# Attention strips: VectorE's instructions in another order, and one quad's values copied by VectorE in place of ScalarE

## The reference

```
xn   = layernorm(x) * g + b                      # over 48 channels, then shifted by 3 and cut into windows
q, k, v = xn @ qkv_w + qkv_b                     # per window: 49 x 16 for each of 3 heads
attn = softmax(q k^T / 4 + rel_bias)             # 49 x 49 per head
out  = (attn v) @ proj_w + proj_b
x    = x + shift_back(out)                       # first residual
h    = gelu(layernorm2(x) @ fc1_w + fc1_b) @ fc2_w + fc2_b
x    = x + h                                     # second residual
```

## Time and profile before

| | |
|---|---|
| median of 3 runs | 1924.59 us (1921.74 to 1933.83) |
| the profiled execution | 1921.47 us, its span 1919.8 us |
| PE, PEld busy | 1733.5 us (90%), 1054.6 us (55%) |
| DVE busy | 1597.7 us (83%) |
| ACT busy | 1535.9 us (80%) |
| POOL busy | 1244.9 us (65%) |
| mean granted TensorE clock | 0.961 |

### The profile page before, as it was taken

How to read it: one execution, slowest core, us unless ns; L and a number is a source line. 1 busy time by engine, 2 the same in 40 slices (tenths; PEclk the granted TensorE clock), 3 DMA queues, 4 the chain that set the end, 5 groups by cost and what they waited for, 6 DMA issues and landing times. The chain is left out here.

```text
span 1919.8 us, 90636 instructions
## 1 busy us (share of the span) xinstructions
PE 1733.5 (90%) x38184; PEld 1054.6 (55%) x38184; DVE 1597.7 (83%) x2140; ACT 1535.9 (80%) x3090; POOL 1244.9 (65%) x1048
## 2 busy tenths in 40 slices
PE   5899999999999999999999999986999958998996
PEld 3566656565666656666665656651697943333332
DVE  6899889998999999999989899854777757888883
ACT  3788888888888888888888888875666639888891
POOL 5788888888888888888888888762355540221222
PEclk9999999999999999999999999995899975999998
DMA  4343554444443444444344444322588849999994
GB/s 116 89 115 97 152 133 115 106 107 115 100 116 99 117 102 113 109 105 113 98 116 102 117 105 106 85 59 67 134 217 215 216 119 170 245 260 253 253 268 142
DMA packets 233230, 262.27 MB, mean 137 GB/s; under 512 B 167078, under 2 KB 179910, under 8 KB 232710
## 3 DMA queue, kind: packets, MB, share of 16 engines
q1 hardware_dynamic: 217478, 217.48, 47.4%
q0 software_dynamic: 15360, 39.08, 6.8%
HBM read 160.81 MB, written 80.88 MB: 126 GB/s over the span
## 5 line engine op out<-in xcount | busy, mean ns | idle before, releaser
L425 POOL TENSOR_TENSOR shift<-const_b,qmax 113x588 bf16<-113x588 bf16 x256 | 414.1, 1618 | 214.7 <-DVE qmax L520 214.7
L512 DVE TENSOR_TENSOR Ul<-Uf 113x784 bf16<-113x784 f32 x192 | 259.8, 1379 | 0.0
L1501 POOL DMA_DIRECT2D out_rolled<-r_OUT x128 | 64.0, 504 | 268.2 <-DVE r_OUT L1601 268.2
L520 DVE TENSOR_REDUCE qmax<-ps_s 113x12 f32<-113x588 f32 x256 | 195.4, 763 | 50.3 <-PE ps_s L917 46.6
L1347 PE MATMUL conv_ps<-xin,band_now 64*64 64x448 bf16 x2688 | 203.4, 365 | 2.2 <-DVE x_low L1242 2.2
L731 ACT ACTIVATE P<-ps_t 113x588 f32<-113x588 f32 x256 | 170.0, 664 | 36.6 <-PE ps_t L969 34.3
L724 ACT COPY Uf<-ps_m 113x392 f32<-113x392 f32 x384 | 172.8, 485 | 28.7 <-PE ps_m L882 20.8
L1347 PE MATMUL conv_ps<-x_low,band_now 64*64 64x448 bf16 x1344 | 178.1, 352 | 0.0
L741 ACT COPY V<-ps_t 49x192 f32<-49x192 f32 x512 | 169.1, 330 | 9.2 <-PE ps_t L969 3.0
L984 PEld LDWEIGHTS ps_o<-P,V 113*32 113x32 f32 x6144 | 107.8, 109 | 102.7 <-ACT P L731 53.0
L762 ACT ACTIVATE G<-ps_m 128x392 f32<-128x392 f32 x256 | 113.9, 502 | 44.5 <-PE ps_m L1023 44.2
(11 more groups left out here) (246 smaller groups left out, 5339.9 us busy)
## 6 DMA issues: line engine op xcount, KB each, us to landing
xin<-rows_scratch SPq DMA_DIRECT2D x96, 236.0 KB, 3.7
XT<-x_tokens SPq DMA_DIRECT2D x64, 294.0 KB, 3.5
X<-x_windows SPq DMA_DIRECT2D x128, 147.0 KB, 3.4
RS<-rs_scratch SPq DMA_DIRECT2D x128, 147.0 KB, 3.2
XR<-x_windows SPq DMA_DIRECT2D x128, 147.0 KB, 3.2
x_scratch<-x SPq DMA_DIRECT2D x128, 147.0 KB, 3.5
y_scratch<-y POOLq DMA_DIRECT2D x96, 196.0 KB, 2.8
r_RS<-rs_scratch SPq DMA_DIRECT2D x128, 147.0 KB, 4.8
```

What stands on the lines that cost most here:

```text
L425: nc.gpsimd.tensor_tensor(shift[:, j % 2], e, m, ALU.mult).then_inc(S["md"], 1)
L512: nc.vector.tensor_tensor(Ul[:, r, h, :], Uf[:, r, h, :], U[0][:, r, h, :], ALU.subtract).then_inc(S["u_lo"], 1)
L520: nc.vector.tensor_reduce(qmax[:, j % 2, :].rearrange("p (b n) -> p b n", b=2), ps_s[0:R, :, 0:2 * HQ].rearrange("p b (n t) -> p b n t", t ...
```

## The change

ScalarE no longer calls `keep_values(s, 2)`, the copies of quad 2 (the third quad). VectorE makes the same two copies in a new `keep_third(s)`, right behind `divide(s, 0)`, counted by a semaphore of their own, `vev_third`; ScalarE's `exp_scores(s, 2)` waits for it, and TensorE's two waits on copied values are split between the two semaphores by `kept`. On VectorE, `u_low(nxt, 1)` moves from ahead of `subtract_mean(prv)` to behind `square(prv)`, and `u_low(nxt, 2)` from ahead of `query_max(nxt, 1)` to behind it. The number of instructions of every kind stays the same over all engines together.

```diff
--- before.py
+++ after.py
@@ -238,11 +238,15 @@
         x2_margin = sem("x2_margin")
         margins_stored = sem("margins_stored")
         names = ("t_sum t_mean t_cen t_sqr t_var t_ln t_rs xh0 lo0 uu u_hi u_lo s_q mx kb md st ex vev pv lnd rdn nrm "
-                 "proj x1_made x1_lo cen xc sq sq_lo var ln rs xh1 lo1 f1 ge f2 x1_biased x2_made").split()
+                 "proj x1_made x1_lo cen xc sq sq_lo var ln rs xh1 lo1 f1 ge f2 vev_third x1_biased x2_made").split()
         S = {nm: sem(f"{nm}_done") for nm in names}
 
         def halves(ap):
             return ap.rearrange("p (b n) -> p b n", b=2)
+
+        def kept(q):
+
+            return (S["vev"], 2 * (q // 4 * 3 + (0, 1, 2, 2)[q % 4])), (S["vev_third"], 2 * (q // 4 + (q % 4 > 2)))
 
         def of_kind(ap, a):
             return ap.rearrange("p (j a t) -> p a j t", a=2, t=2 * TOK)[:, a]
@@ -522,6 +526,15 @@
                         ps_s[0:R, :, 0:2 * HQ].rearrange("p b (n t) -> p b n t", t=TOK),
                         AX_X, ALU.max).then_inc(S["mx"], 1)
 
+            def keep_third(s):
+
+                if s.real:
+                    q = 4 * s.n + 2
+                    wait(dve, S["st"], q + 1)
+                    wait(dve, S["pv"], q - 1)
+                    for p in range(2):
+                        nc.vector.tensor_copy(*kept_values(p, 2)).then_inc(S["vev_third"], 1)
+
             def divide(s, j):
 
                 if s.real:
@@ -602,14 +615,15 @@
                 first_residual(prv)
                 normalise1(old)
                 divide(s, 0)
+                keep_third(s)
                 u_low(nxt, 0)
-                u_low(nxt, 1)
                 subtract_mean(prv)
                 query_max(nxt, 0)
                 divide(s, 1)
                 square(prv)
+                u_low(nxt, 1)
+                query_max(nxt, 1)
                 u_low(nxt, 2)
-                query_max(nxt, 1)
                 add_bias(prv)
 
             def clear_inputs(tiles, r):
@@ -727,6 +741,8 @@
                 if s.real:
                     q = 4 * s.n + j
                     wait(act, S["st"], q + 1)
+                    if j == 2:
+                        wait(act, S["vev_third"], 2 * (s.n + 1))
                     wait(act, S["pv"], q - 1)
                     nc.scalar.activation(P[:, j % 2].rearrange("p (b n) h t -> p b n (h t)", b=2),
                                          ps_t[0:R, :, 0:2 * SV].rearrange("p b (n c) -> p b n c", c=SV)[:, :, :, 0:HQ],
@@ -784,7 +800,6 @@
                 invert_sums_end(s, 0)
                 u_high(nxt, 2, 0)
                 u_high(nxt, 2, 1)
-                keep_values(s, 2)
                 exp_scores(s, 2)
                 token_root(s.at(3))
                 invert_sums(s, 1)
@@ -930,7 +945,8 @@
                     if j == QUADS // 2:
                         wait(pe, swapped[s.slot(2)], 64 * (s.turn(2) + 1))
                     wait(pe, S["ex"], q)
-                    wait(pe, S["vev"], 2 * q)
+                    for copied in kept(q):
+                        wait(pe, *copied)
                     r = s.slot(2)
                     for k in range(2):
                         for n, (ws, ms) in enumerate(((0, 0), (0, 1), (1, 0))):
@@ -975,7 +991,8 @@
                 if s.real:
                     q = 4 * s.n + j
                     wait(pe, S["ex"], q + 1)
-                    wait(pe, S["vev"], 2 * (q + 1))
+                    for copied in kept(q + 1):
+                        wait(pe, *copied)
                     wait(pe, S["nrm"], q)
                     for k in range(QP):
                         at = TOK * (k ^ j // 2 * 2)
```

## The result

The changed kernel takes 1968.93 us (median of 4 runs, 1966.93 to 1970.53) against 1926.94 us before (median of 4, 1921.74 to 1933.83, the runs made beside it included). The ratio is 1.0218 with a 95% interval of 1.0196 to 1.0241: slower, by 42 us; the interval leaves open whether by more than 2%. The forecast was 1957 us.

The account below looks back on a forecast made before the run. No engine has room, so the loop closing a step (19.68 us), with two equally long branches, bounds the kernel. A step of 20.23 us, +0.55 over about 60 steps, adds 33 us: 1957 us, range 1896 to 1975.

Parts of the forecast that it names:

- The two levers: What sets the step: VectorE's mean subtraction (early is good, forecast 0.73 us earlier) and the second residual (late is bad).
- the likeliest case: Main forecast: last low part and add_bias wait for GpSimd, step 20.23 us, 1957 us, range 1940 to 1975; chance 0.56.
- the other branch: Equally long loop branch: second residual, fourth quad's division, projection; residual forecast to start at 621.18 instead of 620.01.
- All three cases: VectorE/GpSimd turns: GpSimd 0.22 us ahead wins; 0.11 ahead, VectorE wins two instructions; 0.3 behind first of two, GpSimd goes between.
- Rival 1: On VectorE, add_bias goes ahead of GpSimd's low0: step 19.27 us, 1900 us in all, faster; chance 0.20.
- Rival 2: VectorE's last low part slips ahead of GpSimd's squares_low: step 19.00 us, 1884 us in all, faster; chance 0.06.
- Rival 3: Issue order alone decides VectorE/GpSimd turns, so make_shift beats the square: +20 us, 1945 us in all; chance 0.04.
- Rival 4: Mixture: L491 is beaten again, step 19.8 us, or strips alternate between both patterns: 1915 to 1940 us; chance 0.14.
- The copies: Third quad's two copies on VectorE behind the division: 0.62 to 0.70 us, hidden under GpSimd's low1.
- the 1.4 of the bound: Upper limit for the two copies on VectorE, in us; would add some 17 us in all through a later exponential.
- What is late next: Chain from second residual to projection: shrinks from 5.06 to 4.38 us, with the projection starting at 625.56.
- my sum: Whole kernel: step 20.23 against 19.68 us, +0.55 us over about 60 steps, +33 us.

Follow-up runs that it names:

- experiment 5: Changed kernel with the two third-quad copies exchanged, partitions 64 to 112 first: 1964.03 us, ratio 1.0204 to the kernel before.
- Experiment 1: Changed kernel with its last u_low moved back ahead of the second maximum: 1893.86 us, ratio 0.9836 to the kernel before.
- experiment 8: Changed kernel with add_bias moved ahead of the last low part: 2072.08 us, ratio 1.0741 to the kernel before.
- experiment 2: Kernel before with only VectorE's low-part order changed, copies left on ScalarE: 1965.26 us, ratio 1.0198.
- experiment 3: Changed kernel with the low parts in the old order, so only the copies moved: 2073.52 us, ratio 1.0755 to the kernel before.
- experiment 4: Changed kernel without add_bias and the wait on it (fc2's bias left out): 1925.15 us, ratio 1.0004 to the kernel before.
- experiment 9: Changed kernel with the old low-part order in its first three steps only: 1963.22 us, ratio 1.0192 to the kernel before.
- experiment 6: Kernel before with one low part ahead of the subtraction, two behind the square before the second maximum, copies on ScalarE: 1898.61 us, ratio 0.9853.
- experiment 7: Changed kernel with last u_low ahead of the second maximum and the two copies exchanged: 1889.66 us, ratio 0.9819 to the kernel before.

## Why the prediction was right

**The two levers.** Right in kind, and 1969 us lies in the likeliest case's own range of 1940 to 1975. The subtraction came earlier by 0.57 us against the division and fc1 by 0.56, where 0.73 was forecast: 0.11 of the difference is the hold that experiment 5 takes away, 0.05 is low1, which starts 0.64 us behind the division instead of 0.59. Experiment 1 shows that this travels to the end once the other branch is kept out of the way. The second residual came late, and TensorE's waits for x, for the third division and, with the projection's weight load (0.33 us), for the fourth all follow from it: that division ends at 649.60, the projection starts at 649.65.

**The turns.** All three cases held at their new places: low1 ran in its native 1.49 us under the copies; make_shift, 0.11 ahead of the square, waited through both (2.99 again); squares_low, 0.23 ahead, made the last low part 2.09 us long (2.1 was said); low0 took 2.22 and add_bias 1.85, the figures that were put down. Rival 1 (a tensor_scalar might go ahead) is refuted by the changed kernel itself and, from the other side, by experiment 8. Rival 2 fell with the 0.23 us. Rival 3, issue order alone, fell with the 2.99 of make_shift: there the Trainium skill ("SBUF — State Buffer", "Who interferes with whom") and the measurement differ, and the measurement decides. The rows give recorded starts, and an offset between those of the two engines, somewhere from 0.11 to 0.22 us, would reconcile the first of the two VectorE instructions with issue order, but not the second: that low part starts 0.99 us behind make_shift and still goes first. Rival 4 fell too: no mixture is seen in steps that are 20.34 or 20.35. Experiments 2, 3 and 4 separate the three suspects: the order alone costs 39 us, the removal of add_bias brings 44 back, and the copies cost little here (0.11 us a step) although in the old order they cost 148 us, the stretches at half clock included.

**The copies.** 0.74 us, just above the 0.62 to 0.70 that I had and far below the 1.4 of the bound; the exponential starts 1.28 behind the division (1.24 said). They were covered by low1 as argued. What I missed is the 0.11 us behind the low part that follows them.

**What is late next.** From the second residual to the projection 649.65 - 645.33 = 4.32 (4.38 said), with L495 at 0.49 us instead of 1.01 for the reason given.

**The size.** 33 us were forecast and 42 measured between the medians, 47.5 between the profiled executions. Two terms are missing from my sum. The step is 20.34 instead of 20.23: from the division to the second residual it is 11.75 (11.57 said), from there to the projection 4.32 (4.38 said), and on to the next division 4.27 (4.28 said). The first of these holds the 0.11 of VectorE held behind the copy on partition 64, shown by experiment 5 (20.22). Over 60 steps that is 7 us. And I counted only steps, where the fill alone costs 6 (experiment 9). With both, the sum is 46 us for the profiled pair. The medians lie closer since the profiled execution before was 5 us faster than the median of its kernel; I had allowed 3.

**What stays open.** In experiments 1, 6 and 7, and now and then in 4, steps are longer than the plain one, by up to 1.5 us, with the clock at 1.00; in the longest of them TensorE is idle without any semaphore wait that the trace names (20.38 us in experiment 1, with 1.42 of idle time in the middle of one row of score products). The changed kernel has such a pause too, of 0.97 us, in a step that is no longer than the others. Their cause was not tried. Nor was the mechanism by which make_shift, waiting since before the square, is passed over between two VectorE instructions while low0 and low1, issued later against the first of the two, are not; only the pattern is shown.

## What to carry to other kernels

Where VectorE and GpSimd take turns, an instruction's place decides more than its length: list which pairs of starts meet, who waits, and what is queued behind the loser. Let the engine lose that has time (make_shift's 3.87 us cost nothing) and do not put two contending instructions in a row where a queued one of the other engine can go between them and the second of the two is urgent. When a change has an edit that gains and one that loses, run the order and the move apart, and look at the fill of the pipeline by itself.

## What the runs showed of the hardware that was not expected

- Behind VectorE copies that end with the one on partitions 64 to 112, the next instruction (which starts on partition 0) and the next one that reads PSUM start 0.03 to 0.04 us after the end of the one ahead, instead of 0.07 to 0.08 before it (experiment 5): 0.11 us each.
- TensorE's granted clock was 1.00 in the changed kernel's steady steps of 20.34 us (window below; before). In experiments 3 and 8, with full-clock steps of 20.9 to 21.1, it fell again and again to half, 1.2 GHz, and steps with such a stretch took 22 to 24 us. In experiment 3 the full-clock step is 0.8 us longer than the changed kernel's, the average of the 63 steps 1.8 us longer (1384.9 against 1271.7 us in all). The changed kernel's window:

```profile
500.00:700.00 200.00, 184.60 (x4806) 115.84 (x4806) 185.72 (x258) 164.15 (x374) 161.62 (x110) 1.00 0.41 104
```

- Three VectorE instructions in a row can keep GpSimd out: 3.87 us for an instruction of 1.17.
